# Handing the carries of a segmented scan to the groups' first three columns: six operations on 1024 numbers for two on 3072, with a column in front of the ring

## The reference, cut to what matters

```python
h = x[src]; out = segment_sum(h * weight, dst)              # layers 0, 1 and 3 (layer 3 twice)
msg = x[src] @ W + ...; out = segment_max(msg, dst)          # layer 2, four times
```

## Time and profile before

| | |
|---|---|
| median of 3 runs | 10687.7 us (10673.33 to 10689.66) |
| the profiled execution | 10684.92 us, span 10683.1 us |
| POOL busy | 8083.7 us, 76% |
| DVE busy | 4206.9 us, 39% |
| PE, ACT busy | 1642.6 us (15%), 543.4 us (5%) |
| DMA engines, mean | 34.8% (two queues of 19.5% and 15.2%, and 0.1%) |
| L991, the gathers | 5824, busy 6299.6 us, mean 1082 ns |

### The profile page before, as it was taken

How to read it: one execution, slowest core, us unless ns; L and a number is a source line. 1 busy time by engine, 2 the same in 40 slices (tenths; PEclk the granted TensorE clock), 3 DMA queues, 4 the chain that set the end, 5 groups by cost and what they waited for, 6 DMA issues and landing times. The chain is left out here.

```text
span 10683.1 us, 48143 instructions
## 1 busy us (share of the span) xinstructions
PE 1642.6 (15%) x9025; PEld 1443.0 (14%) x9025; DVE 4206.9 (39%) x7872; ACT 543.4 (5%) x1417; POOL 8083.7 (76%) x7137
## 2 busy tenths in 40 slices
PE   2000048888860000100001000100001000010000
PEld 1000047777750000100001000100001000010000
DVE  4333334444443333333333333333334333433334
ACT  2000021111130000000000000000001000000000
POOL 5777768888847777677776777677777777777777
PEclk7555567677775555555555555555555555555555
DMA  5444435555532222322232222322223222322223
GB/s 186 141 141 142 148 88 77 77 77 77 75 86 87 94 94 94 99 94 94 94 101 92 94 94 94 105 88 94 95 94 99 94 94 94 100 94 94 95 94 107
DMA packets 442216, 1064.84 MB, mean 100 GB/s; under 512 B 153734, under 2 KB 273392, under 8 KB 409786
## 3 DMA queue, kind: packets, MB, share of 16 engines
q0 software_dynamic: 320736, 464.07, 19.5%
q1 hardware_dynamic: 118280, 597.44, 15.2%
q10 hardware_dynamic: 2940, 1.00, 0.0%
HBM read 517.80 MB, written 552.72 MB: 100 GB/s over the span
## 5 line engine op out<-in xcount | busy, mean ns | idle before, releaser
L991 POOL DMA_INDIRECT WORK<-table,S x5824 | 6299.6, 1082 | 2042.5 <-issue 1772.1
L1210 POOL DMA_INDIRECT acc<-TOT,stage x832 | 1301.2, 1564 | 275.0 <-issue 207.1
L1045 DVE TENSOR_TENSOR Z<-WORK,RESET 128x1024 f32<-128x1024 f32 (+1 forms) x312 | 375.8, 1204 | 2789.9 <-DMA WORK<-table,S 2782.8
L1090 PE MATMUL bank<-ident,WORK 128*128 128x128 f32 x7 | 3.3, 474 | 8122.2 <-DVE WORK L1074 8122.2
L1045 DVE TENSOR_TENSOR Z<-WORK,KEEP 128x1024 f32<-128x1024 f32 (+1 forms) x234 | 281.8, 1204 | 2094.1 <-DMA WORK<-table,S 2088.8
L1090 PEld LDWEIGHTS bank<-ident,WORK 128*128 128x128 f32 x7 | 1.3, 181 | 8123.7 <-DVE WORK L1074 8123.7
L1048 DVE TENSOR_TENSOR WORK<-WORK,Z 128x1024 f32<-128x1024 f32 (+1 forms) x546 | 657.5, 1204 | 18.8
L1059 DVE TENSOR_TENSOR Z<-WORK,S 128x384 f32<-128x384 f32 (+3 forms) x273 | 610.2, 2262 | 6.3
L1064 DVE TENSOR_TENSOR WORK<-WORK,Z 128x384 f32<-128x384 f32 (+3 forms) x273 | 606.1, 2247 | 6.3
L1415 DVE SCALAR_TENSOR_TENSOR BASE<-bank,WEIGHT,BASE 128x128 f32<-128x128 f32 x832 | 234.0, 344 | 766.8 <-PE bank L1285 714.1
L1053 DVE SCALAR_TENSOR_TENSOR WORK<-WORK,S 128x128 f32<-128x128 f32 x1428 | 502.5, 352 | 51.1
(11 more groups left out here) (247 smaller groups left out, 2654.5 us busy)
## 6 DMA issues: line engine op xcount, KB each, us to landing
run_rows<-WORK SPq DMA_DIRECT2D x175, 2048.0 KB
WORK<-table,S POOLq DMA_INDIRECT x5824
fill_rows<-BASE SPq DMA_DIRECT2D x52, 1024.0 KB
WORK<-fill_rows SPq DMA_DIRECT2D x104, 512.0 KB
table<-TF SPq DMA_DIRECT2D x56, 384.0 KB
WORK<-carry_rows SPq DMA_DIRECT2D x49, 384.0 KB
acc<-TOT,stage POOLq DMA_INDIRECT x832
acc<-Z SPq DMA_DIRECT2D x12, 1024.0 KB
```

The lines of the kernel that those rows point to most:

```text
L991: pool.indirect_dma_start(RING_T[:, b * WIDE + k, :], None, table, table_row(table, INDEX[:, t:t + 1]))\
L1045: step(dve.tensor_tensor(TMP[:, 0:groups, 0, :], rows[:, :, j - 1, :], mask(keep[:, :, j], groups, 0), op0))
L1210: pool.indirect_dma_start(acc_dram[a], bass.IndirectOffsetOnAxis(stage[:, h, j % HALF:j % HALF + 1].bitcast(u32), 0), TOT[:, j // QUAD % 2 ...
```

## The change

- L1059 and L1064 are replaced by a loop over j = 0, 1, 2: for each j one operation on 1024 numbers from the groups' carries and PREFIX into TMP, and one from TMP into column j of the groups. Six operations per chunk, in even chunks too; each waits for the one before it.
- WORK gets one column more, BEFORE, in front of the ring. ENDS is WORK seen from that column on, so that the last column of the group before is at a constant stride for the first group too. At the start of each even chunk but the first, a new `tensor_copy` of 128 numbers puts the ring's last column into BEFORE.
- POOL's wait ahead of a chunk's last column: for even chunks it is for the whole chunk before, as it was; for odd chunks it is for the copy alone.
- TMP shrinks from 3072 to 1024 numbers; `carried` moves from a tile of its own into Z. `done` counts the new steps. A second wait on the gathers inside the loop over the groups goes.

```diff
--- before.py
+++ after.py
@@ -144,10 +144,9 @@
         zeros = Z[:, 0:HALF * F]
         neutral = sb("neutral", [2, F])
         no_node = sb("no_node", [1, BLOCK])
-        WORK = sb("WORK", [P, 4 * HALF * F])
-        RUN = WORK[:, :].rearrange("p (b t f) -> p b t f", b=BUFS, t=HALF)
-        CARRY = WORK[:, 4 * HALF * F - NT * F:].rearrange("p (t f) -> p t f", f=F)
-        FILL = WORK[:, 2 * HALF * F:].rearrange("p (h t f) -> p h t f", h=2, t=HALF)
+        WORK = sb("WORK", [P, (SPAN + 1) * F])
+        CARRY = WORK[:, 4 * HALF * F - NT * F:SPAN * F].rearrange("p (t f) -> p t f", f=F)
+        FILL = WORK[:, 2 * HALF * F:SPAN * F].rearrange("p (h t f) -> p h t f", h=2, t=HALF)
         ACC = WORK[:, 0:2 * ACCS * GROUP * F].rearrange("p (s k t f) -> p s k t f", s=2, k=ACCS, t=GROUP)
 
         def field(k, dt=f32):
@@ -179,7 +178,6 @@
         stage = sb("stage", [P, BUFS, HALF], i32)
         G = Z[:, HALF * F:HALF * F + 8 * F].rearrange("p (a f) -> p a f", f=F)
         carry_t = sb("carry_t", [P, 2, P])
-        carried = sb("carried", [P, F])
         unset = sb("unset", [P, F])
         NR = sb("NR", [P, 2, GROUP, F])
         FE = sb("FE", [P, 2, GROUP, F])
@@ -223,8 +221,11 @@
 
         INDEX = S[:, 0:T].bitcast(i32)
         PREFIX = S[:, T:2 * T]
-        TMP = Z[:, 0:3 * GROUPS * F].rearrange("p (g j f) -> p g j f", g=GROUPS, j=3)
-        RING_T = WORK[:, :].rearrange("p (t f) -> p t f", f=F)
+        TMP = Z[:, 0:GROUPS * F].rearrange("p (g f) -> p g f", g=GROUPS)
+        carried = Z[:, HALF * F:(HALF + 1) * F]
+        RING_T = WORK[:, F:].rearrange("p (t f) -> p t f", f=F)
+        BEFORE = WORK[:, 0:F]
+        ENDS = WORK[:, 0:SPAN * F].rearrange("p (t f) -> p t f", f=F)
 
         banks = [ctx.enter_context(nc.psum_tensor(f"bank{i}", [P, 1024], f32)) for i in range(4)]
 
@@ -969,16 +970,13 @@
             parts = (((0, WIDE - HALF),) if WIDE > HALF else ()) + tail
             stored_all = [16 * len(range(b, LAST, RING)) + (16 * len(parts) if LAST % RING == b else 0)
                           for b in range(RING)]
-            steps = 6 + GROUPS + 2
+            steps = 12 + GROUPS
 
             def done(c, n=WIDE):
 
                 if c < LAST:
-                    return (c + 1) * steps + (c + RING - 1) // RING * 2 + (2 if c % RING == 0 else 0)
-                before = done(c - 1)
-                if WIDE > HALF:
-                    before += 6 + HALF // FOUR + 2 + (2 if c % RING == 0 else 0)
-                return before + n - (WIDE - HALF)
+                    return (c + 1) * steps + c // RING
+                return c * steps + (c - 1) // RING + 12 + HALF // FOUR + n - (WIDE - HALF)
 
             def pool_part(pool):
                 for c in range(COUNT):
@@ -987,7 +985,7 @@
                     for k in range(WIDE):
                         t = c * WIDE + k
                         if k == WIDE - 1 and c >= RING - 1:
-                            wait(pool, reduced, done(c - RING + 1))
+                            wait(pool, reduced, done(c - 1) if c % RING == 0 else done(c - 2) + 1 if c > 1 else 0)
                         pool.indirect_dma_start(RING_T[:, b * WIDE + k, :], None, table,
                                                 table_row(table, INDEX[:, t:t + 1]))\
                             .then_inc(landed[t // QUAD % len(landed)], 16)
@@ -1011,7 +1009,7 @@
 
             def dve_part(dve, st):
                 dve.memset(unset[:], neutral_value)
-                st.then(dve.memset(RING_T[:, SPAN - 1, :], neutral_value))
+                st.then(dve.memset(BEFORE, neutral_value))
                 if fill:
                     dve.memset(blank, 0.0).then_inc(blanked, 1)
                 if masks is not None:
@@ -1029,39 +1027,36 @@
                 def grid(first, groups):
                     return RING_T[:, first:first + FOUR * groups, :].rearrange("p (g j) f -> p g j f", j=FOUR)
 
-                def mask(m, groups, width):
-                    return m.unsqueeze(len(m.shape)).to_broadcast([P, groups, width, F] if width else [P, groups, F])
+                def mask(m, groups):
+                    return m.unsqueeze(2).to_broadcast([P, groups, F])
 
                 def combine(t0, groups):
 
                     first = t0 % SPAN
                     rows = grid(first, groups)
+                    ends = ENDS[:, first:first + FOUR * groups:FOUR, :]
                     keep = scale[:, t0:t0 + FOUR * groups].rearrange("p (g j) -> p g j", j=FOUR)
                     prefix = PREFIX[:, t0:t0 + FOUR * groups].rearrange("p (g j) -> p g j", j=FOUR)
+                    if first == 0 and t0:
+                        wait(dve, reduced, n)
+                        step(dve.tensor_copy(BEFORE, RING_T[:, SPAN - 1, :]))
                     for t in range(t0, t0 + FOUR * groups, QUAD):
                         arrived(t)
                     for j in range(1, FOUR):
                         wait(dve, reduced, n)
-                        step(dve.tensor_tensor(TMP[:, 0:groups, 0, :], rows[:, :, j - 1, :],
-                                               mask(keep[:, :, j], groups, 0), op0))
+                        step(dve.tensor_tensor(TMP[:, 0:groups, :], rows[:, :, j - 1, :], mask(keep[:, :, j], groups), op0))
                         wait(dve, reduced, n)
-                        step(dve.tensor_tensor(rows[:, :, j, :], rows[:, :, j, :], TMP[:, 0:groups, 0, :], op1))
+                        step(dve.tensor_tensor(rows[:, :, j, :], rows[:, :, j, :], TMP[:, 0:groups, :], op1))
                     for g in range(groups):
                         last = first + FOUR * g + FOUR - 1
                         wait(dve, reduced, n)
-                        arrived(t0)
-                        step(dve.scalar_tensor_tensor(RING_T[:, last, :], RING_T[:, (last - FOUR) % SPAN, :],
-                                                      prefix[:, g, FOUR - 1:FOUR], RING_T[:, last, :], op0, op1))
-                    wait(dve, reduced, n)
-                    spans = [(0, groups)] if first else [(0, 1), (1, groups)]
-                    for a, b in spans:
-                        ends = RING_T[:, (first + FOUR * a - 1) % SPAN:, :][:, 0:FOUR * (b - a - 1) + 1:FOUR, :]
-                        step(dve.tensor_tensor(TMP[:, a:b, :, :],
-                                               ends.unsqueeze(2).to_broadcast([P, b - a, 3, F]),
-                                               mask(prefix[:, a:b, 0:3], b - a, 3), op0))
-                    wait(dve, reduced, n)
-                    for a, b in spans:
-                        step(dve.tensor_tensor(rows[:, a:b, 0:3, :], rows[:, a:b, 0:3, :], TMP[:, a:b, :, :], op1))
+                        step(dve.scalar_tensor_tensor(RING_T[:, last, :], ends[:, g, :], prefix[:, g, FOUR - 1:FOUR],
+                                                      RING_T[:, last, :], op0, op1))
+                    for j in range(FOUR - 1):
+                        wait(dve, reduced, n)
+                        step(dve.tensor_tensor(TMP[:, 0:groups, :], ends, mask(prefix[:, :, j], groups), op0))
+                        wait(dve, reduced, n)
+                        step(dve.tensor_tensor(rows[:, :, j, :], rows[:, :, j, :], TMP[:, 0:groups, :], op1))
 
                 for c in range(LAST):
                     combine(c * WIDE, GROUPS)
```

## The result

The changed kernel takes 10713.3 us (median; 10709.9 to 10720.2) where the kernel before, on the same chip, takes 10686.0 (10673.3 to 10696.0). The ratio is 1.0027, interval 1.0019 to 1.0034: slower by 0.27%, where 6.1% faster was predicted. The profiled execution is 10713.01 us, its span 10711.2.

The account below looks back on a forecast made before the run. POOL's row of gathers, stretched by DVE's long operations, was taken to bound the kernel. The gain was 760 - 117 + 8.5 = 651 us, so 10687.7 - 651 = 10036.7 us, range 9950 to 10125.

Parts of the forecast that it names:

- The loss rule: A gather starting beside a long DVE operation loses the operation's end, less the gather's start, less 0.13 us.
- B: Six new operations in a row hold a gather to the sixth's end: 447 us lost, 11135 us; chance 0.03.
- C: New phase passes gathers only at every second boundary: 4.40 us per chunk against 4.34, 10689 us; chance 0.02.
- A: DVE's offset against POOL in the new phase comes out otherwise: 9929 to 10137 us; chance of further off 0.09.
- Rival D: DVE doesn't stretch the gathers; their transfers or rows do, long gathers stay, 10687.7 us; chance 0.02.
- DVE's added time: Six operations per chunk lengthen DVE's phases by 115 us in all, hidden in DVE's idle time.
- The copy and POOL's two waits in the chunk: Copy into BEFORE taken as 0, at most 18 us; POOL's wait before a last column never bound, worth 0.
- the first one: A pass is a row of 832 gathers on POOL, one per 1.248 us when free, with DVE following.
- the 760 us of losses: Removing the chunks' long DVE operations frees POOL's gathers: 4.90 us per odd chunk, 3.83 per even, 760 together.
- The sum's other terms (117 and 8.5 us): 117 us lost to the six new operations in the chunks; 8.5 us gained in the last chunk's first half.
- The prediction's last sentence: Signs of failure: gathers above 2 us, POOL waiting for `stored` or `reduced`, or short gathers pitched above 1.25 us.
- Waits and stores at 0: POOL's waits, stores, moved `carried`, smaller TMP and dropped second waits cost 0; a store keeps 10 us of slack.

Follow-up runs that it names:

- e1: Changed kernel without the six operations that hand the carries to the groups' first three columns; 10716.6 us, ratio 1.0029 to the kernel before.
- e2: Changed kernel with one DVE memset of 128 numbers per chunk in place of the chunk's reduction; 10713.4 us, ratio 1.0027 to the kernel before.
- e4: Changed kernel with one more POOL wait per pass, ahead of chunk 13, until chunk 12 is reduced; 10726.5 us, ratio 1.0038.
- e5: Changed kernel with gathers of 64 rows instead of 128; 10712.4 us (one execution).
- e7: Changed kernel with one more POOL wait per pass, ahead of chunk 24, until the chunk before is reduced; 10726.3 us, ratio 1.0042.
- e9: Kernel before with the changed form only in chunks 0 to 3 of each pass; 10726.1 us, ratio 1.0040.
- e13: Kernel before with the changed form only in chunks 19 to 22 of each pass; 10638.8 us, ratio 0.9968.
- e15: Kernel before with forty ScalarE copies per chunk, gathers replaced by plain one-column loads from SP; 6686.6 us (one execution).
- e16: Kernel before with forty ScalarE copies per chunk, gathers replaced by plain four-column loads from SP; 6341.1 us (one execution).
- e3: Changed kernel with forty one-number memsets on DVE added behind each chunk's reduction but the last; 11355.0 us, ratio 1.0623.
- e8: Changed kernel with forty one-number copies on ScalarE added after each chunk but the last; 10844.7 us, ratio 1.0153.

## Why the prediction was wrong, point by point

**The loss rule held.** L1057 ends at 9999.51 + 1.22 = 10000.73 and the gather beside it at 10001.55, 0.82 later; rule and rows gave a gather of 1.56 and then 0.95, the trace 1.55 and 0.95. The long gathers are gone (median 948, longest 1992 ns in the last pass, for 3700). Rivals B and C, that the boundary isn't a door or is one only every second time, are out by these rows, and A by the offset (0.49 for the 0.47 taken). Two even chunks were to be 81.6 us apart; in the last pass chunks 2 and 4 (counted from 0) start at 9558.68 and 9640.35, 81.7 apart.

**Rival D is out too.** The Trainium skill, page "SBUF — State Buffer", section "Who interferes with whom", has it that a `tensor_tensor` was not seen to stall DMA. In these traces the gathers beside one end 0.82 us behind its end, and change with its length (3.70 us beside one of 3.36 in before, 1.55 beside one of 1.22 in after); the traces disagree with that sentence. What D would have given, no change in time, is near the result, but for another reason.

**DVE's added time hid, as said**: busy rose by 123.8 us (about 100 was given), and e1, without the six operations, is no faster. **The copy and POOL's two waits in the chunk cost 0**, also as said: no wait for `stored` or `reduced` shows at L989. (The time given until the ring's half is wanted again should have been 40.8 - 17.4 - 0.75 = 22.7 us and not 22; nothing hangs on it.)

**The step that failed is the first one**: that a pass is a row of 832 gathers, each free to start 1.248 us after the last, taken from 20 gathers between two operations of DVE. Twenty is about what the stock holds, and before never emptied it. The pitch that lasts is 1.40 us, and 832 x 1.40 = 1165 us less some 19 x 1.40 = 27 is the 1138 us that after, e1, e2, e4 and e5 all have. Before stood at 1153: of the 760 us of losses only 7 x 15 = 105 lay above that floor. The sum's other terms (117 and 8.5 us) were right in kind and had nothing left to act on. The rows of before did hold a hint: its mean pitch, 1151.8 / 831 = 1.386, is below 1.40 by a hundredth, so with the stock nothing in it was held, but nothing in it showed 1.25 over more than a chunk either. The prediction's last sentence named the sign ("the gathers are short but their pitch rises above 1.25 us") and gave it no price.

**Waits and stores at 0 failed as well**, at a place that the prediction didn't look at: behind the pass. With POOL's stock used up, the runs' ends take longer (87.1 us for 75.2; e2, whose DVE is all but empty, has the same 117 us between passes, with 5.9 of wait and 96.7 of run ends), and DVE's stock, smaller by six more instructions per chunk, spreads its last eleven operations over 13.7 us in place of 4.3. The two overlap in part: e1 and e2 have none of the second and the same time. Six times 21.1 us and 6.1 behind the last pass are the 127 and 6 of the ledger, more than the 105 won. Behind the last pass only the wait for the store grows (12.2 us for 5.8); the runs' ends take 73.6 us there for before's 73.8, so a used-up stock doesn't slow the 49 gathers themselves. What grows is POOL's wait for DVE, which waits for TensorE's results. That it comes and goes with POOL's stock is shown by e7; how, is not.

So a pass and its run ends together are nearly a constant: 1153 + 75 = 1228 before, 1138 + 87 = 1225 after, 1150 + 74 = 1224 in e7, and 1235 in e2 and e9. (832 + 49) x 1.40 = 1233 is near all of them; that the gather that starts early in a pass is borrowed from the ones behind it would fit, but is not shown, as POOL goes at 1.25 us there between its waits. e13 gains on after in both parts: its wait for the last store is before's 5.9 us, and its run ends take 84.9. That this is because it spends the stock just at the end and leaves DVE's nearly full is argued from the table and was not tried by itself.

**What stays open.** What the stock is. On POOL, DVE and ACT it is per engine, counts instructions of 0.06 to 1 us alike, and refills at one per 1.40 us (at times two 0.70 apart). It goes with POOL's gathers in a pass (e15, e16) and holds on for some us behind them, and is not felt in the loop of layer 1, nor by DVE between passes, though POOL issues indirect DMAs in both. What sets the two apart, no run here tells. TensorE was not tried. An estimate: in the stretch shown above it starts 36 instructions from 9389.56 on, weight loads counted, and then 12 more; 20 at once and 16 at 1.40 us would end at 9412.0, and 12 more at 9428.8, which is where DVE and ACT start (9412.77, 9428.11). But before's TensorE starts the same 48 from 9373.74 on and nobody waits for it.

All executions timed here were recorded by the profiler, so none can tell whether the recording has a share in the limit. That after's page lists 47345 instructions and before's 48143 is no sign of it: DVE issues 630 more, and the second waits on the gathers, which the change drops, were 7 x (25 x 8 + 4) = 1428; 1428 - 630 = 798, the whole difference.

## What to carry to other kernels

A free pitch read from some twenty instructions may be a burst: before an engine's losses are counted as time to be won, look for the longest stretch of the trace in which it ran at that pitch, and price the rest at the slowest rate that is known to last. Where many small instructions are put in the place of few large ones beside such a stream of gathers, count instructions per time on each engine (in the passes here one per 1.40 us), not only their busy time. And where a limit has a stock, the gain can come from a few places near the end: here four chunks of 25 gave a faster kernel, all 25 a slower one.

## What was not expected of the hardware

- In a pass, while GpSimd streams gathers, each of three engines starts about one instruction per 1.40 us once a stock is used up (19 to 20 on GpSimd and ScalarE): GpSimd's gathers (e2), VectorE's memsets of 0.06 us (e3), ScalarE's copies of 0.19 us (e8). The stock fills up in idle time at the same rate (7 after 10.45 us).
- It is not so wherever GpSimd issues indirect DMAs: beside layer 1's, one per 1.86 us, VectorE starts an instruction every 0.44 us for 1400 us (before).
- The engines' counts are separate: GpSimd keeps 1.25 us beside a held VectorE (e3), and its passes stay at 1138.8 us beside a held ScalarE (e8).
- Rows and bytes don't enter: 64 rows for 128 leave the 1.40 us (e5). With plain loads of twice the rate ScalarE's 40 copies all go in 3.83 us (e15).
- In the waits it shows as "issue", or names as releaser an operation on the same engine that had already ended ([1.05 <-DVE WORK L1069]).
